# Attention stage of a one-core hybrid-layer kernel: the batch loop written as a hardware loop, and the two outputs of a projection taken in another order

## The reference, cut to what matters

```python
q, k, v = heads(x @ wq.T + bq), heads(x @ wk.T + bk), heads(x @ wv.T + bv)
q2, k2 = sum(q * q, -1), sum(k * k, -1)
d2 = maximum(q2[..., :, None] + k2[..., None, :] - 2.0 * einsum('bhid,bhjd->bhij', q, k), 1e-12)
attn = softmax(-sqrt(d2), -1)
out = einsum('bhij,bhjd->bhid', attn, v)
x = x + (out.transpose(0, 2, 1, 3).reshape(B, N, D) @ wo.T + bo)
```

## Time and profile before

| | |
|---|---|
| median of 3 runs | 2578.05 us |
| profiled execution | 2586.95 us, span 2585.2 us |
| busy over the span | PE 86%, DVE 69%, ACT 54%, POOL 45% |
| instructions | 54149 |
| attention stage, from its first clamp to its last | 890 us to 1572 us |
| one batch in it | 87 to 88 us |
| granted TensorE clock | 0.957 of full speed, mean of the span |

### The profile page before, as it was taken

How to read it: one execution, slowest core, us unless ns; L and a number is a source line. 1 busy time by engine, 2 the same in 40 slices (tenths; PEclk the granted TensorE clock), 3 DMA queues, 4 the chain that set the end, 5 groups by cost and what they waited for, 6 DMA issues and landing times. The chain is left out here.

```text
span 2585.2 us, 54149 instructions
## 1 busy us (share of the span) xinstructions
PE 2230.3 (86%) x20912; PEld 1620.5 (63%) x20912; DVE 1786.4 (69%) x4432; ACT 1407.6 (54%) x2159; POOL 1157.4 (45%) x1181
## 2 busy tenths in 40 slices
PE   7957777777899889999999887999797979999979
PEld 4535555555798645555555555898566946666659
DVE  6666777677667667777777764896453747767755
ACT  4631222222333278888888886556111566777755
POOL 4338999992101077567766753000463013223220
PEclk9979999899899889999999999999999989999999
DMA  5454445552100121111111210000000000000001
GB/s 176 147 161 154 139 136 141 153 158 73 59 1 13 48 63 56 53 59 60 56 53 59 64 56 17 20 1 1 15 1 14 26 0 1 1 1 1 1 1 66
DMA packets 158718, 148.86 MB, mean 58 GB/s; under 512 B 21440, under 2 KB 141376, under 8 KB 155392
## 3 DMA queue, kind: packets, MB, share of 16 engines
q1 hardware_dynamic: 138704, 105.51, 13.8%
q0 software_dynamic: 3456, 23.07, 2.7%
q10 hardware_dynamic: 16304, 16.83, 2.2%
HBM read 100.51 MB, written 40.63 MB: 55 GB/s over the span
## 5 line engine op out<-in xcount | busy, mean ns | idle before, releaser
L1827 POOL TENSOR_SCALAR a_dist<-a_dist,a_mq 128x512 f32<-128x512 f32 x512 | 355.9, 716 | 111.0 <-ACT a_mq L1764 111.0
L1870 DVE TENSOR_SCALAR_CACHE_REDUCE a_dist<-a_ring 128x512 f32<-128x512 f32 x512 | 332.4, 687 | 84.4 <-PE a_ring L1513 82.7
L1754 ACT ACTIVATE a_pT<-a_psT 128x1024 f32<-128x1024 f32 x256 | 258.4, 1025 | 80.4 <-PE a_psT L1525 71.9
L1525 PE MATMUL a_psT<-ident,a_dist 128*128 128x128 f32 x2048 | 264.1, 275 | 13.9 <-ACT a_pT L1754 13.5
L1525 PEld LDWEIGHTS a_psT<-ident,a_dist 128*128 128x128 f32 x2048 | 233.9, 142 | 46.8 <-issue 27.3
L1748 ACT ACTIVATE a_dist<-a_dist 128x2048 f32<-128x2048 f32 x128 | 236.8, 1903 | 35.9 <-DVE a_dist L1870 33.0
L1513 PE MATMUL a_ring<-a_stack 102*128 102x512 bf16 x512 | 182.2, 394 | 47.4 <-DVE a_raw L1884 23.6
L1513 PEld LDWEIGHTS a_ring<-a_stack 102*128 102x128 bf16 x512 | 47.4, 98 | 214.7 <-DVE a_dist L1870 141.8
L3349 ACT ACTIVATE ds_wtm<-ds_wg,ds_par 128x256 f32<-128x256 f32 x64 | 29.2, 503 | 271.4 <-DVE ds_wg L3479 267.1
L1187 POOL TENSOR_TENSOR c_y<-c_prod 128x1024 f32<-128x1024 f32 x16 | 37.2, 2349 | 266.4 <-DVE c_prod L1221 264.4
L1538 PE MATMUL a_psO<-a_pT,a_va 128*32 128x512 f32 x1024 | 135.1, 604 | 2.3 <-ACT a_pT L1754 2.3
(11 more groups left out here) (451 smaller groups left out, 6311.0 us busy)
## 6 DMA issues: line engine op xcount, KB each, us to landing
a_stack<-a_parts_dram SPq DMA_DIRECT2D x384, 64.0 KB
a_parts_dram<-a_parts SPq DMA_DIRECT2D x32, 384.0 KB, 2.4
bf_w<-in_up_w_dram POOLq DMA_DIRECT2D x10, 1024.0 KB, 9.2
bf_w<-in_down_w_dram POOLq DMA_DIRECT2D x10, 1024.0 KB, 8.8
ds_nbg<-tok_nbk ACTq DMA_DIRECT2D x128, 64.0 KB
feat_v<-di_part SPq DMA_DIRECT2D x16, 256.0 KB, 2.6
tok_nbk<-di_nbk SPq DMA_DIRECT2D x16, 256.0 KB, 3.0
feat_k<-di_part SPq DMA_DIRECT2D x16, 256.0 KB, 3.5
```

Of the source, the lines that this page charges most:

```text
L1525: last = turn(psT[:, u % 2, kb, q * P:(q + 1) * P], dist[:, g % 2, i, q, k * P:(k + 1) * P], core.ident[:])
L1754: a(pT[:, u // 2, u % 2], psT[:, u % 2], ACT.Exp).then_inc(exp_done, 1)
L1827: last = nc.gpsimd.tensor_scalar(d, d, -1.0, mq[:, g % 2, i, q:q + 1], ALU.mult, ALU.add)
L1870: ts(dist[:, gg % 2, i, q, :], ps[:], 1e-12, 3.0e38, ALU.max, ALU.min, accum_out=mq[:, gg % 2, i, q:q + 1]).then_inc(ring_out, 1)
```

## The change

It has two parts. First, `batches` now emits the first batch, a hardware loop (`Fori`) of three passes over a body of two batches, and the last batch. In the loop the batch is `(r, 1)` or `(r, 2)`: `r` lives in a register of each engine, and each value for a wait, each address into `X`, `rstd` and `shift`, and each DRAM address is computed by register instructions. Second, `take_projection` writes `raw` from the bank first, waits for that, and then makes the bf16 part by a copy from `raw`.

```diff
-        def batches(body):
-            for b in range(B):
-                body((None, b), b == 0, b == B - 1)
+        def batches(eng, body):
+            body((None, 0), True, False)
+            with eng.Fori(0, (B - 2) // 2) as r:
+                body((r, 1), False, False)
+                body((r, 2), False, False)
+            body((None, B - 1), False, True)
 ...
-            batches(body)          # each engine: sp, pe, act, pool, dve
+            batches(sp, body)
 ...
                 reach(dve, sq_done, at(own, NPR, p))
                 reach(dve, rest_done, at(own, NPR, p))
                 scale, bias = (-2.0, nbq[:, p:p + 1]) if p < KD else (1.0, bqk[:, 1, p - KD:p - KD + 1])
-                reach(dve, parts_out[p % 2], at(own, 32, 16 * (p // 2)))
-                ts(parts[:, p % 2, 0, :], ps[:], scale, bias, ALU.mult, ALU.add).then_inc(first_done, 1)
                 ts(raw[:], ps[:], scale, bias, ALU.mult, ALU.add).then_inc(ring_out, 1)
                 dve.wait_ge(ring_out, nth(b, ("pj", p)) + 1)
+                reach(dve, parts_out[p % 2], at(own, 32, 16 * (p // 2)))
+                copy(parts[:, p % 2, 0, :], raw[:]).then_inc(first_done, 1)
                 dve.wait_ge(first_done, at(own, NPR, p + 1))
```

More of the change, by code:

```diff
@@ L1715, in _ @@
             pe.wait_ge(ffn.x_done, NT)
-            batches(body)
+            batches(pe, body)
             end = (None, B - 1)
@@ L1782, in _ @@
             act.wait_ge(scaled, 2)
-            batches(body)
+            batches(act, body)
             end = (None, B - 1)
@@ L1843, in _ @@
                 finish_split(None, (None, 0), p)
-            batches(body)
+            batches(pool, body)
             add_bias((None, B - 1))
@@ L2023, in _ @@
             dve.wait_ge(bf.kept, 32)
-            batches(body)
+            batches(dve, body)
             end = (None, B - 1)
```

## The result

The changed kernel takes 2595.6 us in the median of 20 runs (2585.1 to 2610.2), the kernel before 2578.7 us (20 runs, 2568.5 to 2591.4). The ratio is 1.0065, with a 95% interval of 1.0052 to 1.0080: 17 us slower, inside the predicted range but 13 us past the point, and in the case of over 0.5% slower that had a chance of 0.27.

The account below looks back on a forecast made before the run. PE was taken as the bound, busy 80.6 of 87.6 us in a steady attention batch. Terms 0 + 2 + 2 = +4 us on the 2578.05 us median gave 2582 us, range 2566 to 2606 us.

Parts of the forecast that it names:

- the case of over 0.5% slower: Whole kernel: more than 0.5% (13 us) slower than 2578.05 us, chance 0.27.
- Part one: Projections p = 0, 2, 3: writing raw first moves PE's stall to the clamp; 0 us, ends -14 to +4 us.
- 0.61 (from L1889 to the clamp): DVE in a projection: step from the subtraction's start to the next clamp's, kept at 0.61 us in a 1.86 us sum.
- My own sign for the second part: Attention stage: batches 2 to 7 stay within 0.5 us of 87.6 us if register instructions are priced right.
- the upper row for the copy: DVE's copy to bf16 at p = 3: 0.81 us, the median of an existing SBUF copy's row.
- Part two: Register instructions in the loop: 4 exposed per batch at 0.08 us, six batches, +2 us; range 0 to 69.
- R1: PE's ring waits: register instructions not worked off ahead, one in three exposed at 0.08 us, 2603 us; chance 0.19.
- Part three: Two jumps back at the loop body's end: instruction refetch, 1 us each, +2 us; range 0 to 7.
- My sign of a clock that stays full: Ends of the second body: PE pauses 0 to 3.6 us while TensorE's granted clock stays full.
- R4: Loop ends: dearer jumps, 11 us in all, 2589 us; a clock fall would add a few us; chance 0.11.
- SP: SP's run of loads: computed DMA addresses add 0.8 us, hidden by 7.9 us of slack; cost 0.
- My criterion for failing as a whole: Attention stage: batches between jumps, not jumps, carry the difference, or the stage gains over 1.5 us in each batch.

Follow-up runs that it names:

- the copy alone: Kernel before, eight batches still written out, with the new projection (raw first, bf16 part copied from it in SBUF): 1.0041, +11 us.
- the loop alone: Kernel before with the loop over batches 1 to 6 and the old projection (bf16 part first, both from the bank): 1.0169, +44 us.
- the loop with the waits moved ahead: Loop with old projection, DVE's waits for POOL's split and the lengths moved ahead of the projection's first instruction, against the kernel before: 1.0041, +11 us.
- the kernel with 5 waits: Kernel before, written out, with 5 repeated, already met waits put between raw and the subtraction: 1.0003.

## Why the prediction was right and wrong

**What bounds the kernel**: right. PE is the bound, and all losses passed through its waits and its clock.

**Part one, worth 0 us**: wrong in size, and this is the step that failed first. The stall moved from `raw` to the clamp as said, and the copy's 0.43 us at p = 0 and 2 came out. The term that failed is the last of its sum, "0.61 (from L1889 to the clamp)", which I took over from before; it measured 1.24 at p = 0 (1161.60 to 1162.84). I asked what POOL does to the copy and not what it does to the subtraction behind it, which reads two tiles of SBUF; releasing POOL earlier than the subtraction starts made it 1.31 to 1.41 us. The part is worth 1.17 us in a batch, 7 us in the trace (the copy alone: +11 us by timing). My own sign for the second part, batches within 0.5 us of 87.6, failed by this part and not by the second. At p = 3 the upper row for the copy, 0.81 us, was no bound: a hold can last 3.6 us.

**Part two, +2 us**: right for the changed kernel. With the new projection a batch without jump takes 88.77 us in the loop and 88.76 written out, so its register instructions (32 ns each on PE, 40 on DVE) cost nothing there. The reason I gave, that few are exposed, was only half of it. In the old projection the same instructions cost more than the jumps, since 0.2 us turned the order of two engines. R1's argument, that a register instruction behind a wait cannot start before the wait ends, is what delayed the subtraction in the loop alone; but the delay itself is small, and it has no word of the turned order, which made 2619 us of it and not R1's 2603. The change's own part one hides this cost, as there the square is first in any case.

**Part three, +2 us**: the mechanism was right, the size off. The fetch from nothing, put at 3.6 us, measured 3.9 and 3.4 us of branch. The cover, put at 1 to 2.4 us, measured 1.1, its lower end. 3.6 less these covers is 1.2 to 2.6 us a jump, and I had taken 1, leaning on the jumps forward of the earlier trace rows, which say nothing of a jump back; PE stood for 2.98 and 2.44 us, and the period behind a jump grew by 4.7 us (by 3 to 6 in the traces of other kernels with the loop, where no other hold falls in it). My sign of a clock that stays full failed: a stretch of 3.4 us at the 1.2 GHz level follows eight of the eleven jumps traced directly. R4 named both, at 7 us for two jumps and "a few us more" for the clock.

**SP, 0**: right; the run of loads is 0.6 us longer and PE does not wait for a stack.

**Sum**: parts of +7, 0, +9.5 and 10 us for two held copies, against 0, 2, 2 and nothing. That makes 26 us in the trace; the timing says 17 us (13 to 21), and holds that vary from run to run would fill the gap, which is not shown.

My criterion for failing as a whole, that the batches between the jumps, and not the jumps, carry the difference, was met for the larger part: 7 and 10 of the 26 us. That 2595.6 us lies inside the range is luck. The range reached to 2606 us for the sake of R1, and register instructions, R1's cause, cost the changed kernel's batches nothing.

## What to carry to other kernels

Before an instruction of VectorE with SBUF operands is put behind one that releases GpSimd, look which of the two starts first, to a few hundredths of a microsecond: the trace shows both starts, and the second one ends only when the first has ended and most of its own time has passed. A delay of 0.1 to 0.2 us that looks free, a wait or a register computation, can turn that order and cost ten times its length (3 us against 33 between the loop alone and the loop with the waits moved ahead). To get a bank free early without that, put work that reads PSUM between the release and the SBUF work; here it kept all three instructions at their shortest, though a steady batch gained only 0.1 us by it.

## What the runs showed of the hardware

Two single instructions of the two engines exclude each other on these tiles, and the first one wins: subtraction at 1.54 and square at 1.61 give 0.69 and 1.52 us; subtraction at 1.70 and square at 1.61 give 1.50 and 1.04 us. The second one ends later than the first by nearly its own time: the subtraction (0.69 us alone) by 0.55 us, the square (1.04 us alone) by 0.90. The Trainium skill (SBUF — State Buffer, Who interferes with whom) has this as its rule: a VectorE instruction with two SBUF inputs contends with GpSimd's reads, and issue order decides who blocks. For two single instructions the traces agree.

What I had not expected is that a hold can span many instructions of GpSimd, of which all but the first start after VectorE's. In the kernel with 5 waits, whose instructions start when those of before do, one batch of seven had this at p = 3, in DVE's and POOL's timelines:

```profile
1102.75 3.82 DVE L1890 TENSOR_TENSOR a_rest<-a_raw,a_parts 128x512 f32<-128x512 f32 x1
...
1094.26 10.77 POOL L1827 TENSOR_SCALAR a_dist<-a_dist,a_mq 128x512 f32<-128x512 f32 x16
1104.98 1.05 POOL L1805 TENSOR_TENSOR bf_up<-a_raw 128x512 f32<-128x512 f32 x1
```

POOL's run took 10.77 us for 16 subtractions, 0.67 each. DVE's subtraction came 0.44 us behind the start of the 13th and waited for three more and for the square, until POOL paused; the batch took 92.6 in place of 87.6 us. The order of the starts does not decide this case: three subtractions and the square started behind VectorE's instruction and went first. In five others it came at the same point, 0.43 to 0.45 us behind the start of one, got in behind it and was over in 0.8 us, while POOL's next took 1.12 us. The phase of the two engines doesn't decide between the two, then, and what does is open. The kernel before has the same rows and no hold in its trace; its 20 runs lie 23 us apart, and the part ahead of the stage, which varies by 18.5 us between the traces, can explain most of that; whether holds add to it, nothing here shows.

A taken branch back cost PE 3.4 to 3.9 us in each of the loops traced, eleven times in six traces, and under 0.1 us on the four other engines, whose bodies are shorter (in one pass the trace has 642 records of DVE and 2461 of PE). Each time a packet of 16 KB of the queue that fetches instructions starts 0.9 to 1.4 us behind the start of PE's branch. A packet of 8 KB starts 1.0 to 1.3 us behind the start of DVE's, without a pause of DVE. The Trainium skill (Runtime: NRT & Kernel Launch, Instruction fetch mechanics) says that a taken branch out of the window forces a fetch before the engine goes on. For PE the traces agree; on the other engines no such stall is seen.
